# An eighth unit of seven products, two stored low parts, and three pieces of work moved, in a two-layer graph network on one core

## The reference

```python
# layer 0
deg = adj.sum(1, keepdims=True) + 1e-5
out = (adj / deg) @ x @ W_neigh.T + b_neigh + x @ W_self.T + b_self
x = layernorm(x + relu(out))
# layer 1
d = where(rowsum > 0, rowsum ** -0.5, 0)
out = (d[:, None] * adj * d[None, :]) @ x @ W + b
x = layernorm(x + relu(out))
```

## Time and profile before

| | |
|---|---|
| time, median of 3 runs | 776.54 us (776.53 to 777.35) |
| the profiled execution: time, span | 776.1 us, 774.4 us |
| granted clock of TensorE, mean | 0.998 |
| TensorE: matmuls, busy | 766.6 us, 99% |
| VectorE, ScalarE busy | 720.0 us (93%), 429.5 us (55%) |
| VectorE busy, layer 0, blocks 3 to 6 | 47.1 of 49.6 us each |
| VectorE busy, layer 1, blocks 1 to 6 | 41.6 to 42.0 of 45.1 us each |
| moved by DMA | 161 MB, 208 GB/s over the span |
| layer 0 ends, layer 1's block 0 ends (TensorE) | about 404 us, about 448 us |
| chain that ended last | TensorE 98%, VectorE 1%, ScalarE 1% |

### The profile page before, as it was taken

One profiled execution on the slowest core, in us unless ns is written; L12 is line 12 of the kernel. 1 busy time (PEld: TensorE's weight loads), 2 busy tenths in 40 slices (PEclk: granted clock), 3 DMA queues, 4 the chain that ended last, 5 costly groups with the idle time before them and its releaser, 6 DMA issues.

```text
span 774.4 us, 12666 instructions
## 1 busy us (share of the span) xinstructions
PE 766.6 (99%) x4151; PEld 662.6 (86%) x4151; DVE 720.0 (93%) x1226; ACT 429.5 (55%) x594; POOL 2.5 (0%) x14
## 2 busy tenths in 40 slices
PE   9999999999999999999999999999999999999996
PEld 6888888888888888888888889899898989989896
DVE  6999999999899899998989899898989989898996
ACT  5644645646446364454554755665565566656663
POOL 0000000000000000000000000000000000000000
PEclk9999999999999999999999999999999999999999
DMA  7975574655646547474574756656565665756651
GB/s 302 346 237 195 191 264 155 243 187 200 234 154 244 189 168 266 135 267 168 176 260 147 243 178 208 216 195 241 172 228 198 215 217 176 257 165 229 204 190 61
DMA packets 54206, 161.09 MB, mean 208 GB/s; under 512 B 5024, under 2 KB 18080, under 8 KB 54176
## 3 DMA queue, kind: packets, MB, share of 16 engines
q1 hardware_dynamic: 45680, 151.54, 55.9%
q10 hardware_dynamic: 8352, 9.05, 3.7%
q0 software_dynamic: 144, 0.13, 0.2%
HBM read 152.31 MB, written 8.39 MB: 208 GB/s over the span
## 4 chain that ended last, share of the span: by engine, by line
PE 98%; DVE 1%; ACT 1%; issue 0%; ACTq 0%
PE ps_main L1100 72%; PE ps_epi L979 7%; PE ps_epi L1047 7%; PE ps_main L1038 4%; PE ps_main L1047 2%; PE ps_epi L1038 2%; PE ps_main L979 1%; PE ps_main L1075 1%; PE ps_main L1122 1%; PE ps_main L1060 1%; PE ps_epi L1132 0%; ACT hi L359 0%; ACT xt_sb L382 0%; ACT tt L406 0%; DVE tt L618 0%; PE ps_epi L1000 0%
## 5 line engine op out<-in xcount | busy, mean ns | idle before, releaser
L359 ACT ACTIVATE hi<-raw 128x1024 fp32r<-128x1024 f32 x254 | 254.9, 1013 | 134.5 <-PE ps_main L1100 86.9
L562 DVE TENSOR_TENSOR lo<-raw,hi 128x1024 fp32r<-128x1024 f32 x254 | 296.7, 1170 | 22.5 <-ACT hi L359 22.0
L1100 PE MATMUL ps_main<-hi,xs 128*128 128x512 f32 x1120 | 278.8, 391 | 0.0
L1100 PEld LDWEIGHTS ps_main<-hi,xs 128*128 128x128 f32 x1120 | 207.4, 188 | 41.7 <-issue 0.5
L1100 PE MATMUL ps_main<-lo,xs 128*128 128x512 f32 x560 | 149.7, 389 | 0.0
L853 DVE TENSOR_TENSOR acc<-acc,raw 128x1024 f32<-128x1024 f32 x112 | 136.4, 1218 | 0.0
L1100 PE MATMUL ps_main<-hi,zs 128*128 128x512 f32 x504 | 125.6, 391 | 0.0
L1100 PEld LDWEIGHTS ps_main<-lo,xs 128*128 128x128 f32 x560 | 105.1, 188 | 21.9
L1100 PEld LDWEIGHTS ps_main<-hi,zs 128*128 128x128 f32 x504 | 92.2, 188 | 17.6
L359 ACT ACTIVATE xs<-acc 128x1024 fp32r<-128x1024 f32 (+1 forms) x52 | 54.6, 1050 | 69.3 <-DVE acc L746 55.8
L1047 PE MATMUL ps_epi<-xs 128*128 128x256 f32 x423 | 69.7, 283 | 0.0
(11 more groups left out here) (158 smaller groups left out, 814.8 us busy)
## 6 DMA issues: line engine op xcount, KB each, us to landing
raw<-adj_t SPq DMA_DIRECT2D x256, 512.0 KB, 3.3
res<-x_nat SPq DMA_DIRECT2D x11, 512.0 KB, 5.3
xt_sb<-xt SPq DMA_DIRECT2D x8, 512.0 KB, 5.1
x_scratch<-tt ACTq DMA_DIRECT2D x8, 512.0 KB, 3.8
res<-x_scratch SPq DMA_DIRECT2D x8, 512.0 KB, 4.8
out<-tt ACTq DMA_DIRECT2D x7, 512.0 KB, 4.9
tt<-x_nat SPq DMA_DIRECT2D x3, 512.0 KB, 4.7
acc<-x_nat ACTq DMA_DIRECT2D x1, 512.0 KB, 5.0
```

Of the source, the lines that this page charges most:

```text
L359: return act.activation(dst, src, ACT.Copy)
L562: return dve.tensor_tensor(dst, src, hi_part.bitcast(f32), ALU.subtract)
L1100: last = pe.matmul(ps[:, f, :], stationary(layer, part, jt, f), mov[:, slot(u), cols], start=(jt == 0 and i == 0), stop=(jt == JT - 1 and ...
```

## The change

- `SU` gets unit 4 for blocks 1 to 6: eight units of seven products instead of seven. Block 7 keeps its five (`SU_LAST`). The third of the three places for the split sums moves from `xs` to the weights of layer 0, which are free by then.
- The sums of z are made for eight units, in four whole sets; sets three and four stand one unit sooner (`T_UNITS`).
- `lo` of units 6 and 10 of blocks 1 to 6 (`KEPT`) is stored to DRAM in layer 0, from SyncE's queue behind the raw load of the unit four further on, and loaded again in layer 1, behind the raw load of the unit three further on, after a wait for `hi` of the kept unit. VectorE leaves these two splits out in layer 1 and writes one element instead to signal; in layer 0 it waits for the store before it overwrites the slot. TensorE waits for the load (`lo_full`).
- `z_lo` of tiles 0, 1 and 2 stands one place sooner: at the last place of unit 14 and the first two of unit 15.
- The copy of block 7's sums (`take_own`) moves from the start of `last_epilogue` to behind hi of unit 15, ahead of the last two norm tiles and the store of block 6's rows.

```diff
-SU = (1, 5, 7, 9, 11, 12, 13)
+SU = (1, 4, 5, 7, 9, 11, 12, 13)
+SU_LAST = (1, 5, 7, 9, 11)
+KEPT = (6, 10)
+NK = len(KEPT)
-T_UNITS = (4, 6, 9, 11)
+T_UNITS = (4, 6, 8, 10)
...
+        lo_dram = nc.dram_tensor("lo_scratch", [NB - 1, NK, P, UW], f32, kind="Internal").ap()
...
-            return tuple(u for u in SU if u < TAIL) if is_last(b) else SU
+            return SU_LAST if is_last(b) else SU
+
+        def kept(b):
+            return () if isinstance(b, int) else KEPT
+
+        def kept_in_slot(u):
+            return [v for v in KEPT if slot(v) == slot(u)]
+
+        def kept_count(b, u):
+            per_block = len(kept_in_slot(u))
+            return (b * per_block + (kept_in_slot(u).index(u) + 1 - per_block)) * 16
+
+        def lead(v):
+            return 1 if v == 2 else max(v - 2, 0)
...
+        def s_part(part, b, u):
+            s = s_place(b, u) % SRING
+            if s == SRING - 1:
+                return (wn, ws)[part][:, :, :, :].rearrange("p a k f -> p (a k f)")
...
                     sp.dma_start(raw[:, slot(u), :], adj_in[b, u]).then_inc(raw_full[slot(u)], 16)
+                    if layer == 0 and u - RING in kept(b):
+                        sp.dma_start(lo_dram[b - 1, KEPT.index(u - RING)], lo[:, slot(u), :].bitcast(f32))\
+                          .then_inc(lo_stored[slot(u)], 16)
+                    if layer == 1 and is_first(b) and u == NU - 1:
+                        for v in KEPT:
+                            sp.wait_ge(lo_stored[slot(v)], len(kept_in_slot(v)) * (NB - 2) * 16)
+                    if layer == 1 and u - RING + 1 in kept(b):
+                        v = u - RING + 1
+                        sp.wait_ge(h_ready, g0 + (v + 1))
+                        sp.dma_start(lo[:, slot(v), :].bitcast(f32), lo_dram[b - 1, KEPT.index(v)])\
+                          .then_inc(lo_full[slot(v)], 16)
...
+                    if layer == 1 and is_last(b) and u == NU - 1:
+                        take_own(b, parity)
                     if layer == 1 and is_first(b) and u in T_UNITS:
                         t_hi(T_UNITS.index(u))
...
-                take_own(NB - 1, 1)
                 stationary_hi(0)
...
-                if v == 15 and layer == 0:
-                    z_lo(n, e, p)
-                    if p == 2:
-                        z_lo(n, e, 3)
+                if layer == 0 and (v, p) in ((14, 2), (15, 0), (15, 1), (15, 2)):
+                    z_lo(n, e, ((14, 2), (15, 0), (15, 1), (15, 2)).index((v, p)))
...
-                        split_lo(lo[:, slot(u), cols], raw[:, slot(u), cols], hi[:, slot(u), cols]).then_inc(l_ready, 1)
+                        if layer == 0 and u - RING in kept(b):
+                            dve.wait_ge(lo_stored[slot(u)], kept_count(b, u - RING))
+                        if layer == 1 and u in kept(b):
+                            dve.memset(marks[:, 2:3], 0.0).then_inc(l_ready, 1)
+                        else:
+                            split_lo(lo[:, slot(u), cols], raw[:, slot(u), cols], hi[:, slot(u), cols])\
+                                .then_inc(l_ready, 1)
...
-                        ahead = [v for v in by_seven(layer, b) if max(v - 2, 0) == u]
-                        slot_taken = u in SU and u + 1 in SU
+                        units = by_seven(layer, b)
+                        ahead = [v for v in units if lead(v) == u]
+                        slot_taken = ahead and len([v for v in units if u <= v < ahead[0]]) == 2
...
-                        if i == 2:
+                        if i == 2 and layer == 1 and u in kept(b):
+                            pe.wait_ge(lo_full[slot(u)], kept_count(b, u))
+                        elif i == 2:
                             pe.wait_ge(l_ready, g0 + (u + 1))
```

More of the change, by code:

```diff
@@ L129, in build @@
         tt_stored = sem("tt_stored")
+        lo_stored = [sem(f"lo_stored{s}") for s in range(RING)]
+        lo_full = [sem(f"lo_full{s}") for s in range(RING)]
         ones_set = sem("ones_set")
@@ L194, in by_seven, with s_place @@
                 return ()
-            return tuple(u for u in SU if u < TAIL) if is_last(b) else SU
+            return SU_LAST if is_last(b) else SU
[8 more added lines that the diff above has]
+            return 1 if v == 2 else max(v - 2, 0)
+        def s_place(b, u):
+            return by_seven(1, b).index(u)
         def tile_sums(layer, e, parity, t):
@@ L209, in s_index, with s_sums_of, s_sum @@
         def s_index(b, u):
[L211 to L223, removed]
+            return b * NS + (s_place(b, u) - NS)
+        def s_sums_of(b, parity, u):
+            return acc[:, (s_place(b, u) + NS * (1 - parity)) % 2, :]
+        def s_sum(b, parity, u, i):
+            return s_sums_of(b, parity, u)[:, i * HB:(i + 1) * HB]
+        def s_part(part, b, u):
+            s = s_place(b, u) % SRING
+            if s == SRING - 1:
+                return (wn, ws)[part][:, :, :, :].rearrange("p a k f -> p (a k f)")
+            at = S_AT + s * 4 + part * 2
             return xs[:, at:at + 2].rearrange("p a c f -> p (a c f)")
@@ L392, in s_hi @@
                 act.wait_ge(s_ready, s_index(b, u) + 1)
-                split_hi(s_part(0, u), s_sums_of(parity, u)).then_inc(sh_ready, 1)
+                split_hi(s_part(0, b, u), s_sums_of(b, parity, u)).then_inc(sh_ready, 1)
             def square_tiles(layer, e, parity, pair):
@@ L734, in s_sums @@
                 _, a22, a11, a21 = [raw[:, slot(u), i * HB:(i + 1) * HB] for i in range(4)]
-                s1, s2, s3 = [s_sum(parity, u, i) for i in range(3)]
-                if SU.index(u) >= 2:
+                s1, s2, s3 = [s_sum(b, parity, u, i) for i in range(3)]
+                if s_place(b, u) >= 2:
                     dve.wait_ge(sl_ready, g - 1)
@@ L745, in s_last_sum @@
                 dve.wait_ge(s_chain, s_index(b, u) * 3 + 3)
-                dve.tensor_tensor(s_sum(parity, u, 3), raw[:, slot(u), 0:HB], s_sum(parity, u, 1), ALU.subtract)\
+                dve.tensor_tensor(s_sum(b, parity, u, 3), raw[:, slot(u), 0:HB], s_sum(b, parity, u, 1), ALU.subtract)\
                     .then_inc(s_ready, 1)
@@ L750, in s_lo @@
                 dve.wait_ge(sh_ready, s_index(b, u) + 1)
-                split_lo(s_part(1, u), s_sums_of(parity, u), s_part(0, u)).then_inc(sl_ready, 1)
+                split_lo(s_part(1, b, u), s_sums_of(b, parity, u), s_part(0, b, u)).then_inc(sl_ready, 1)
             def epilogue(layer, e, parity, v, p):
@@ L1044, in seven_products @@
                         pe.wait_ge(sl_ready, s + 1)
-                    mov = s_part((0, 0, 1)[i], u)
+                    mov = s_part((0, 0, 1)[i], b, u)
                     for n, (ps, st, at) in enumerate(summed):
```

## The result

The changed kernel takes 778.62 us (median of 9 executions, 778.01 to 780.59), the kernel before 776.68 on the same chip (9, 776.08 to 777.49). The ratio is 1.003, with a 95% interval of 1.0021 to 1.0039: slower by 0.3%, 1.9 us at the medians. The prediction was 778.4.

A forecast was written before the change was run, and what follows sets the result against it. TensorE's own work bounds the kernel, until the closed VectorE-ScalarE loop loses its small lead. -1.3 + 3.5 - 0.3 = +1.9 us on 776.1 gives 778.0, set to 778.4 for the runs' median; range 775.0 to 780.2.

The forecast's parts named there:

- 2.02 + 1.23 = 3.25: Join of column sums, from block 1: 2.02 us VectorE delay out of block 0, 1.23 for added sums ahead of it.
- +0.05 on top: VectorE in blocks 1 to 6: added sums and split less the two removed lo splits, net +0.05 us a block.
- 0.77 and 0.4: Layer 1's block 0: TensorE stalls 0.77 us for hi at unit 11 and 0.4 for z at unit 15.
- 8.02 + 1.14 - 0.27 = 8.89: Start of unit 5's low part after the join: 8.02 us before, plus unit 4's split 1.14, less 0.27 for narrower lo.
- TensorE waiting for a DMA: Sign that the forecast is wrong; the loads of lo were expected to be hidden, the second barely.
- 3.5 - 1.3 - 0.3 = +1.9: Whole kernel: TensorE stalls 3.5 us, less 1.3 saved by six added seven-product units and 0.3 by the earlier copy.
- the copy's 0.3: Program end: copying the last block's sums straight behind hi 15 removes TensorE's 0.3 us wait.
- rival D: Loads of lo late on top, or raw tiles pushed back by traffic: 1 to 3 us more, 779.5 to 781.5; chance 0.12.
- B: Rival for blocks 1 to 6: the lead lasts and only the gains 1.3 + 0.3 count, 774.9 us; chance 0.10.
- C: Rival, block 0: hi 11 not late because ScalarE reaches its split sooner; 777.6 us, or 776.4 without slip; chance 0.21.
- My margin for lo 10: Layer 1 load of lo 10: issued 19.1 us after the join, lands by +24.4, wanted at +24.5; barely hidden.
- D's other half: Stores and loads push the raw tiles back; within the rival of 1 to 3 us more, whose whole chance was 0.12.

The follow-up runs named there:

- e4: Changed kernel with the third and fourth sets of z's sums a unit later, where they were before: 778.25 us, ratio 1.0020.
- e5: Changed kernel with the sets of z's sums where they were and block 0's memset of PSUM behind the last z tile: 777.72 us, ratio 1.0013.
- e7: Changed kernel with unit 8 instead of unit 4 as the eighth unit of seven products: 779.26 us, ratio 1.0031.
- e3: Kernel before with only the z tiles and the copy of the last block's sums moved: 776.39 us, ratio 0.9994.
- e6: Changed kernel with lo of unit 8 kept in DRAM as well, so three units kept: 777.09 us, ratio 1.0004.
- e1: Changed kernel with no low part kept in DRAM; VectorE computes lo of units 6 and 10 again: 790.68 us, ratio 1.0177.
- e2: Changed kernel with seven units of seven products and z's sets as before, both low parts still stored and loaded: 776.50 us, ratio 0.9997.
- e9: Changed kernel with the two loads of lo issued one raw load sooner: 781.24 us, ratio 1.0059.

## Why the prediction was right

**The mechanism.** The joins say it as forecast: relative to the mark, the join of block 1 stands at 455.32 - 407.07 = 48.25, before at 451.62 - 406.52 = 45.10. That is 3.15 later, and I had 2.02 + 1.23 = 3.25. The period from block 1 to 6 is 45.42, before 45.41, forecast +0.05 on top. So the loop's period was as before, only its place was later, and TensorE, which got quicker, came upon it in block 3.

**Block 0.** ScalarE's timeline in the kernel after (split of the last set, second square, hi of unit 11), and TensorE's weight loads of units 11 and 15:

```profile
432.19 1.06 ACT L400 ACTIVATE xs<-acc 128x1024 fp32r<-128x1024 f32 x1 [3.67 <-DVE acc L763]
...
433.65 0.46 ACT L441 ACTIVATE ps_epi<-tt,nmean 128x256 f32<-128x256 f32 x1
...
434.14 1.04 ACT L400 ACTIVATE hi<-raw 128x1024 fp32r<-128x1024 f32 x1
```
```profile
435.30 1.68 PEld L1149 LDWEIGHTS ps_main<-hi,zs 128*128 128x128 f32 x8 [0.86 <-issue]
...
446.48 1.69 PEld L1149 LDWEIGHTS ps_main<-hi,xs 128*128 128x128 f32 x8 [0.41 <-DVE xs L718]
```

hi 11 starts at 434.14, which is 433.59 in times of the kernel before (less the 0.55 by which layer 1 starts later here); forecast 433.60. The wait of 0.86 is put down to "issue", yet it ends with hi 11 (434.14 + 1.04 = 435.18): e4, where hi 11 starts at 430.46, hasn't got it. Forecast were 0.77 and 0.4, measured 0.86 and 0.41.

**Blocks 1 to 6.** VectorE in block 3 (low part of unit 4's sums, of unit 5's, the marker in place of lo 6):

```profile
552.13 1.22 DVE L604 TENSOR_TENSOR xs<-acc,xs 128x1024 fp32r<-128x1024 f32 x1
...
555.13 1.22 DVE L604 TENSOR_TENSOR ws_sb<-acc,wn_sb 128x1024 fp32r<-128x1024 f32 x1
...
557.03 0.06 DVE L867 MEMSET marks<- 128x1 f32 x1
```

Unit 5's low part starts 8.88 after the join; 8.02 + 1.14 - 0.27 = 8.89 were reckoned. TensorE's side of the same block:

```profile
549.86 0.30 PEld L1026 LDWEIGHTS ps_epi<-xs,st_hi 128*128 128x128 f32 x2 [0.29 <-DVE st_lo L604]
...
552.26 0.19 PEld L1085 LDWEIGHTS ps_epi<-lo,zs 128*128 128x128 f32 x1 [0.20 <-DVE lo L604]
...
556.41 0.19 PEld L1094 LDWEIGHTS ps_main<-ws_sb,zs 128*128 128x128 f32 x1 [0.25 <-DVE ws_sb L604]
```

I had looked for all of it at unit 5. In blocks 3 and 5 some falls at the product behind unit 3 and at lo 4 instead, which were as tight; the same is true of one load of lo (0.20 in block 6). Forecast for blocks 1 to 6 were 2.3 us, measured 2.2 in nine waits of 0.2 to 0.3. With block 0 the total is 3.5, as forecast. The prediction had named "TensorE waiting for a DMA" as a sign of being wrong. By its letter that sign came, at 0.2 us; in this kernel it is a small part, in e4, e5 and e7 it is not.

**The sum.** 3.5 - 1.3 - 0.3 = +1.9; the length of layer 1 says +1.75, the medians +1.9. The +1.9 of both is closer than the parts were known: the copy's 0.3 is at most 0.2 in e3's length and isn't resolved in its time. The added units save what was reckoned: e6, with only the 1.3 us of waits in block 0, has a layer 1 shorter by 0.4 than before, for 1.3 + 0.3 - 1.3 = 0.3. The stores are free: VectorE has no wait for one. One sum was a little off: the units as priced add up to 45.0 us a block and not 45.1. The leads were reckoned with 45.12, and that is what the trace before has, in six periods from the first product with the weights in block 1, at 458.48, to that in block 7, at 729.20. e1, e2 and e6 refute rival D as far as the traffic goes; the joins, 3 us later, refute B. C (hi 11 not late) would have given 777.6 or less; hi 11 started within 0.01 us of the forecast.

**What the prediction had too simply.** It treated the loads of lo as one wait of at most 1 us, "once, not per block". e4, e5 and e7 wait five and six times for them. A load that SyncE issues when VectorE is done with the lo before it belongs to the same late loop, with 4.7 us of landing behind it (median); it was a second limit within a few tenths of the first, and in the changed kernel it was hidden by the waits ahead of it. My margin for lo 10 (lands by +24.4, wanted +24.5) had said that much. And D's other half, raw tiles pushed back, is a real mechanism with a price (e9: +3.2), which the change avoids by its place in the queue.

The Trainium skill (VectorE: DVE Perf Modes, The DRAIN you can't avoid) would have made each added sum 0.42 and the loop 0.15 a block longer than mine. The same section adds that an instruction which isn't held starts earlier, and that is the part which the trace bears out. The sums for unit 7 in block 3 of the kernel after start 0.33 to 0.34 us apart at 0.42 each, and the period grew by 0.01:

```profile
554.13 0.42 DVE L781 TENSOR_TENSOR acc<-raw 128x256 f32<-128x256 f32 x1
554.47 0.42 DVE L782 TENSOR_TENSOR acc<-raw 128x256 f32<-128x256 f32 x1
554.80 0.42 DVE L784 TENSOR_TENSOR acc<-raw,acc 128x256 f32<-128x256 f32 x1
```

The N/2.4 + 2.5 ns that the prediction took from the Trainium skill (TensorE: Matmul & The Clock Gate, Back-to-back issue gap) is given there for an isolated matmul, so it says little of the stream of a unit. The prediction did well to let the rows decide: 0.22 us a unit, and e6 fits that.

What stays open: why profiled executions enter layer 1 up to 1.5 us apart with the same code in layer 0. It may be all that lies between e5 and the changed kernel, whose medians are 0.9 apart with a layer 1 of the same length: their profiled spans are 0.9 apart too (775.8, 776.7), and their marks 0.8 (406.25, 407.07). One trace of each can't show it.

## What to carry to other kernels

Before adding work to an engine that never makes the bottleneck wait, measure its lead at one marker per iteration and its period against the bottleneck's: here 0.1 to 1.6 us of lead and a period longer by 0.3, in a kernel in which TensorE never waited. In that state each microsecond added to the loop costs about one at the end (e1: 6 x 2.05 = 12.3 us put in, 12.1 lost), and one taken off repays only if nothing else stands within a few tenths (e4, e5, e7). The order within the block decides where the wait falls; e7, with another order of the same work, took as long. A transfer added in front of another in one queue delays the consumer of the other; look for its wait on the engine that isn't the bottleneck.

## What the runs showed of the hardware

Transfers of 512 KB more in the queue came with longer landings of their neighbours: raw tiles land in 3.8 us (median) in the kernel after, 3.3 before, with 224 GB/s moved over the span for 208. e1 and e3, which move nothing more, have 3.3 as well. The stores take 4.8, the loads of lo 4.7:

```profile
raw<-adj_t SPq DMA_DIRECT2D x256, 512.0 KB, 3.8
lo_scratch<-lo SPq DMA_DIRECT2D x12, 512.0 KB, 4.8
lo<-lo_scratch SPq DMA_DIRECT2D x12, 512.0 KB, 4.7
```

I had not expected that 0.5 us on the median raw tile would cost nothing, and that one place in the queue would cost 3 (e9).
